# RWKV time mixing and a mixture of experts on one core: the first chunks' preparation put in another order

## What is computed

```python
h  = layernorm(x)
xk = h * mix_k + last(h) * (1 - mix_k)        # last: the token before; xv and xr likewise
k, v, r = xk @ Wk.T, xv @ Wv.T, xr @ Wr.T
wkv = wkv_log_space(exp(time_decay), time_first, k, v)   # a scan over the tokens of a sequence
x = x + layernorm((wkv * sigmoid(r)) @ Wo.T)
h2 = layernorm(x)
x = x + layernorm(routed(h2) + shared(h2))    # the best 2 of 8 experts, and a shared gated expert
```

## Time and profile before

| | |
|---|---|
| median of 3 runs | 1613.29 us (1612.08 to 1614.66) |
| the profiled execution | 1613.5 us, of which the span of its instructions is 1611.7 us |
| PE busy | 1518.8 us (94%) |
| DVE, ACT, POOL busy | 1377.9, 1335.3 and 1082.7 us (85%, 83%, 67%) |
| mean granted TensorE clock | 0.974 |

### The profile page before, as it was taken

How to read it: one execution, slowest core, us unless ns; L and a number is a source line. 1 busy time by engine, 2 the same in 40 slices (tenths; PEclk the granted TensorE clock), 3 DMA queues, 4 the chain that set the end, 5 groups by cost and what they waited for, 6 DMA issues and landing times.

```text
span 1611.7 us, 35130 instructions
## 1 busy us (share of the span) xinstructions
PE 1518.8 (94%) x9960; PEld 1363.9 (85%) x9960; DVE 1377.9 (85%) x3140; ACT 1335.3 (83%) x2768; POOL 1082.7 (67%) x1168
## 2 busy tenths in 40 slices
PE   4899999999999999999999999689999998999992
PEld 3778888888888888888888888578999998999992
DVE  4799999999999999999989988856877777999993
ACT  3688898889888998999899888756777777999993
POOL 1146767767776777677667766756666664888886
PEclk9899999999999999999999999879999999999996
DMA  3112533343322222222322222228778763777771
GB/s 112 53 47 78 169 107 125 116 153 121 109 88 87 85 78 92 87 82 80 104 76 88 81 81 69 68 79 284 237 241 249 238 217 123 233 232 228 234 236 55
DMA packets 124619, 214.41 MB, mean 133 GB/s; under 512 B 19975, under 2 KB 67338, under 8 KB 124432
## 3 DMA queue, kind: packets, MB, share of 16 engines
q1 hardware_dynamic: 92368, 126.13, 26.5%
q0 software_dynamic: 32064, 86.04, 14.5%
HBM read 116.37 MB, written 99.39 MB: 134 GB/s over the span
## 4 chain that ended last, share of the span: by engine, by line
PE 61%; POOL 16%; issue 11%; DVE 5%; ACT 2%; DMA 1%; POOLq 0%; DVEq 0%; ACTq 0%; SPq 0%
PE PS L1453 51%; POOL d_ys L589 8%; POOL out L607 6%; PE PS L1445 3%; PE PS L1517 2%; PE PS L1515 2%; PE PS L1671 2%; POOL rsw L601 1%; PE PS L1687 1%; POOL d_xd L548 1%; DMA out<-vv,wqh 0%; POOL varw L599 0%; DVE st L1060 0%; PE PS L1652 0%; PE PS L1537 0%
## 5 line engine op out<-in xcount | busy, mean ns | idle before, releaser
L548 POOL DMA_INDIRECT d_xd<-h2n,ixs x248 | 312.0, 1258 | 193.8 <-DVE h2n L1178 127.6
L1453 PE MATMUL PS<-hTh,wqh 128*128 128x512 f32 x768 | 307.1, 400 | 16.0 <-ACT kk L644 10.8
L1453 PE MATMUL PS<-hTl,wqh 128*128 128x512 f32 x768 | 306.7, 399 | 0.0
L1453 PE MATMUL PS<-hTh,wql 128*128 128x512 f32 x768 | 306.2, 399 | 0.0
L1453 PEld LDWEIGHTS PS<-hTh,wqh 128*128 128x128 f32 x768 | 146.7, 191 | 50.9 <-ACT kk L644 11.7
L1453 PEld LDWEIGHTS PS<-hTh,wql 128*128 128x128 f32 x768 | 146.6, 191 | 34.5
L1453 PEld LDWEIGHTS PS<-hTl,wqh 128*128 128x128 f32 x768 | 146.8, 191 | 33.4
L555 POOL DMA_INDIRECT d_xs<-ysh,ixs x124 | 131.2, 1058 | 45.7 <-issue 45.4
L1687 PE MATMUL PS<-weh,h2h 128*128 x380 | 106.3, 280 | 0.0
L1687 PE MATMUL PS<-weh,h2l 128*128 x380 | 106.3, 280 | 0.0
L1687 PE MATMUL PS<-wel,h2h 128*128 x380 | 106.1, 279 | 0.0
(11 more groups left out here) (328 smaller groups left out, 5715.2 us busy)
## 6 DMA issues: line engine op xcount, KB each, us to landing
xin<-in_L_attn_x SPq DMA_DIRECT2D x32, 512.0 KB, 4.2
x<-in_L_attn_x SPq DMA_DIRECT2D x32, 512.0 KB
wqh<-d_xd SPq DMA_DIRECT2D x60, 272.0 KB, 3.6
wql<-d_xd SPq DMA_DIRECT2D x60, 272.0 KB, 3.4
d_xd<-zt SPq DMA_DIRECT2D x18, 272.0 KB
wel<-in_L_ffn_w SPq DMA_DIRECT2D x16, 256.0 KB, 5.1
d_xd<-h2n,ixs POOLq DMA_INDIRECT x248, 2.5
kk<-d_xs SPq DMA_DIRECT2D x12, 256.0 KB
```

Of the source, the lines that this page charges most:

```text
L548: g.indirect_dma_start(d_xd[s], bass.IndirectOffsetOnAxis(ap=ixs[:, m % 2, k:k + 1], axis=0), h2n_of(m)[:, j, :], None).then_inc(s_sct[s], 16)
L1453: ins = mm_(out_ap, l, r, start=(k == 0), stop=(k == len(todo) - 1))
```

## The change

The instructions and transfers stay the same; only their order on SP, ACT and DVE differs, and the semaphores of two small loads.

- SP: chunk 1's rows are loaded as soon as chunk 0's are scaled, ahead of the wait for the weights (`s_wl` 6) and of `x1` and `wel`.
- ACT: `x_normed(0)` goes to the front, ahead of the three `high_mix`; `posw` and `lowb` go behind `turned_high(0)`. `x_normed(1)` goes ahead of the two waits that end the preparation. The first iterations of the loop are written out: `k_out(0)` no longer stands behind `x_normed(1)`'s place in the loop, and `beta(0)` comes ahead of `v_out(0)`, `turned_high(1)` ahead of `alpha(0)`, `own_exp(0)` and `x_normed(2)`.
- DVE: `omm` waits for its three vectors alone (`s_vec` 48; the other two count on `s_wu`). `stats_in(1)` and `negw` stand behind the last `low_mix`, ahead of the output, gate and down weights. Then `running_max(0)`, `step_up(0)`, `stats_in(2)`, `turned_low(1)`.

PE's and POOL's streams are not touched.

```diff
@@ sync
                 for i, v in enumerate((u_in, decay)):
-                    sp.dma_start(vec[:, 3 + i, :], v.rearrange("(a p) -> p a", p=P)).then_inc(s_vec, 16)
+                    sp.dma_start(vec[:, 3 + i, :], v.rearrange("(a p) -> p a", p=P)).then_inc(s_wu, 16)
...
+            sp.wait_ge(s_nx, n(0, NT, NT))
+            sp.dma_start(xin[:, :, :], x_v[1]).then_inc(s_x, 16)
             sp.wait_ge(s_wl, NP)
             sp.dma_start(x1[:, :, :], x_v[0]).then_inc(s_xr, 16)
...
-                if 0 < i < NCH:
+                if 1 < i < NCH:
                     sp.wait_ge(s_nx, n(i - 1, NT, NT))
                     sp.dma_start(xin[:, :, :], x_v[i]).then_inc(s_x, 16)
@@ scalar
-            act.wait_ge(s_vec, 16 * 5)
-            A.activation(posw[:, :], vec[:, 4, :], ACT.Exp).then_inc(s_aprep, 1)
             act.wait_ge(s_const, NCONST)
-            copy(lowb[:, :], lowf[:, :]).then_inc(s_aprep, 1)
+            x_normed(0)
             high_mix(0, al)
-            x_normed(0)
             high_mix(1, be)
             high_mix(2, ee)
             turned_high(0)
+            act.wait_ge(s_wu, 16 * 2)
+            A.activation(posw[:, :], vec[:, 4, :], ACT.Exp).then_inc(s_aprep, 1)
+            copy(lowb[:, :], lowf[:, :]).then_inc(s_aprep, 1)
...
             copy(rwp[:, :, 0:RW], rwf[:, :, :]).then_inc(s_aprep, 1)
+            x_normed(1)
 
             act.wait_ge(s_prep, 7)
             act.wait_ge(s_wl, NP)
 
-            for i in range(NCH + 2):
+            k_out(0)
+            A.preload_act_table(ACT.Silu)
+            r_tanh(0)
+            A.preload_act_table_set("natural_log_exp_and_others")
+            beta(0)
+            v_out(0)
+            turned_high(1)
+            alpha(0)
+            own_exp(0)
+            x_normed(2)
+
+            for i in range(3, NCH + 2):
@@ vector
             stats_in(0)
-            dve.wait_ge(s_vec, 16 * 5)
+            dve.wait_ge(s_vec, 16 * 3)
             V.tensor_scalar(omm[:, :, :], vec[:, 0:3, :], -1.0, 1.0, ALU.mult, ALU.add).then_inc(s_prep, 1)
-            dve.wait_ge(s_aprep, 1)
-            V.tensor_scalar(negw[:, :], posw[:, :], -1.0, None, ALU.mult).then_inc(s_prep, 1)
-            dve.wait_ge(s_prep, 2)
+            dve.wait_ge(s_prep, 1)
...
             low_mix(1)
             low_mix(2)
-
+            stats_in(1)
+            dve.wait_ge(s_aprep, 1)
+            V.tensor_scalar(negw[:, :], posw[:, :], -1.0, None, ALU.mult).then_inc(s_prep, 1)
...
-            for i in range(NCH + 2):
+            dve.wait_ge(s_prep, 2)
+            running_max(0)
+            step_up(0)
+            stats_in(2)
+            turned_low(1)
+
+            for i in range(3, NCH + 2):
                 if on(i - 5):
                     route(i - 5)
-                if on(i - 3):
+                if i > 3 and on(i - 3):
                     step_up(i - 3)
```

More of the change, by code:

```diff
@@ L209, in rwkv_moe @@
         s_vec = sem("s_vec")
+        s_wu = sem("s_wu")
         s_rwf = sem("s_rwf")
```

## The result

The changed kernel takes 1603.3 us (median of 5 runs, 1598.54 to 1604.03) against 1613.29 us (5 runs, 1612.08 to 1614.66) before: ratio 0.9931, 95% interval 0.9915 to 0.9947. That is 10.0 us faster; the forecast was 1601.8 with the range 1598.5 to 1605.5. The profiled execution took 1603.3 us.

What follows compares the result with a forecast made beforehand. PE bounds the kernel at 31.83 us per chunk from 138.60 us, so only its earlier start for chunks 0 to 2 counts; the terms sum to 11.5 us won, giving 1601.8 us, range 1598.5 to 1605.5.

Steps and rivals of the forecast that it cites:

- Step 1: Chunk 0's first projection: ACT scales the rows ahead of the weight rounding, so PE begins at 17.73, 0.65 us later.
- Step 2: Chunk 0's V: the 8.53 us wait for `kk` goes, and 2.8 us of half clock behind it.
- Step 3: Chunk 1's low part, queued behind chunk 2's rows and statistics: PE waits 3.65 us instead of 2.00, 1.7 lost.
- the upper row: Bound on chunk 2's rows' landing: 5.5 us, the longest load seen, with a megabyte ahead; the forecast took 3.9.
- chunk 2's rows come late: Rival: rows behind the experts' weights land after 5.5 us, 1.65 lost, 1603.5; first pair late too, 1604.5 to 1608.5; chance 0.16.
- Step 4: Chunks 1 and 2: waits for `rkl` (1.77) and chunk 2's low part (1.19) go; 0.4 lost to half clock.
- a new wait between 64 and 127 us: Sign on PE's timeline, at 64 to 127 us, that the prediction would be wrong.
- The sum: All steps together: -0.65 + 8.53 + 2.8 - 1.7 + 1.77 + 1.19 - 0.4 = 11.5 us won.
- given back: Rival: after chunk 2 PE meets a wait that does not move, so no change, 1613.3; chance 0.07.
- Slower: Rival: chunk 1's rows land after 19.8 us, each microsecond paid; gain gone at 31.3, 1618 at 36; chance 0.04.

Runs made afterwards that it cites:

- experiment 8: experiment 4's kernel with the third mixed weight made ahead of the first weight's low part on DVE; 1597.81 us.
- experiment 3: The changed kernel with chunk 1's low part ahead of chunk 2's statistics on DVE; 1599.9 us.
- experiment 4: The changed kernel with SP loading chunk 2's rows once chunk 1's are scaled, ahead of `x1` and the experts' weights; 1598.47 us.
- 5: The changed kernel with 22 products that nobody reads on PE ahead of chunk 1's projection; 1601.9 us.
- Experiment 6: The changed kernel with 8 products that nobody reads on PE ahead of chunk 0's second turn; 1599.53 us.
- experiment 7: The changed kernel with SP holding chunk 1's rows until the first half of chunk 0's K is done; 1608.35 us.
- experiment 9: The changed kernel once more, word for word, for a second profile; 1603.24 us.
- 1: The kernel before with only SP's early load of chunk 1's rows; 1606.65 us.
- 2: The kernel before with only ACT's and DVE's first loop iterations reordered as in the change; 1605.23 us.
- 10: experiment 8's kernel with 8 unread products on PE in each of two waits, ahead of chunk 1's projection and chunk 0's second turn; 1593.01 us.
- 11: The kernel of experiment 10 with 13 unread identity turns on PE between chunk 0's turn and the first product; 1594.68 us.
- 12: The kernel of experiment 11 once more, word for word; 1593.37 us.

## Why the prediction was right, point by point

**Step 1** (first projection 0.65 later, at 17.73): 17.83. Right, by its own mechanism, as experiment 8 showed by undoing it.

**Step 2** (V without its wait, 8.53 + 2.8): the gap is gone, and with it the half clock behind it. `wdl` starts at 26.82 (predicted 26.89), chunk 1's statistics stand at 19.86 (19.85), `kk` is copied from 27.63 (27.7), chunk 1's turn at 36.09 (36.6). The half microsecond too much is mostly the first projection, which had 7 products at the slow pace of 0.43 us instead of 9 before.

**Step 3** (chunk 1's low part, 1.7 lost) **is the term that was mis-sized**: PE waits 5.84 us where it waited 2.00, 3.8 lost. 0.6 of that is no loss, as chunk 1's turn ended at 37.1 instead of 37.7; the projection started at 42.96 instead of 41.35. The mechanism was the one named, chunk 2's rows behind the experts' weights with the low part behind them, and experiments 3 and 4 show it from both sides. The sizes were off in two places: the rows were issued at 34.76 instead of 34.0, since the first pair of weights took 5.9 us to land (27.94 to 33.84) and not 5.1 as before, and they took 39.55 - 34.76 = 4.8 us instead of 3.9; in experiments 5 to 7 they took 4.6 to 5.0. The prediction took the second pair, issued 0.9 us ahead of the rows, as mostly drained by then. In the window that ends with the rows' issue nothing had moved yet (the last figure is GB/s):

```profile
33.80:34.80 1.00, 1.00 (x6) 0.83 (x5) 0.00 (x0) 0.97 (x2) 0.00 (x0) 1.00 0.00 0
```

So the whole half megabyte was still ahead of them. The 3.87 us of the kernel before was a load with an empty queue, and in experiment 4, where the rows go ahead of the weights, they landed after 3.9 us too; the upper row, 5.5, was nearer. That is the rival "chunk 2's rows come late" at its first price: 1.6 us late at the projection against 1.65, and its time, 1603.5, lies nearer the measured one than the forecast does.

**Step 4** (1.77 + 1.19 won, 0.4 lost): both waits are gone, chunk 2's projection follows the output product without a bracket, and the `kk` wait of chunk 2 stayed (1.99, predicted 2.3). Chunk 1's projection took 19.27 us where 18.8 was taken. By chunk 2's V 10.13 us were won, 1.4 less than the sum of 11.5. A second loss had no term: the 1.88 us at chunk 0's second turn and half the clock behind it took 1.4 more, which leaves 8.73. Experiment 6 gives it back. The prediction's list of waits had no `h2n` in it (0.38 us before), and it had named a new wait between 64 and 127 us as a sign of being wrong: this one grew there.

**The sum** of 11.5 was thus 2.8 too high at the long run in this profile, and 1.5 too high in the second (9.99, experiment 9). The time came within 1.5 us of the forecast since the rest of the span was 1.5 us shorter in this execution; that part was luck and not argument. Of the rivals, "given back" was right in kind: PE, early, met waits that hang on other engines, and paid 1.4 us of clock, not 11. "Slower" had its price right up to chunk 1's projection (6.4 us there for 6.7, experiment 7) and too high behind it (3.9 us), but needed rows that land after 19.8.

## What to carry to other kernels

A wait taken away at the head of a pipe shows the next one in line, so price what each engine's queue holds behind the next transfer, and ask whether the instruction that everybody waits for needs that transfer at all: here one swapped pair of calls, or one load issued earlier, brought chunk 0's second turn 3.3 or 5.5 us forward. Don't take a load's time from a row with an empty queue if weights were issued just ahead of it. Count the clock behind a wait too: here stretches behind waits of 1.9 to 8.5 us cost another 1.3 to 2.8 us, though not every time, and work that nobody reads held the clock wherever it filled the wait. Follow a point such as the first long run's start, since the rest of the time changed by up to 4.7 us between executions, and take the clock's part out of that point as well before comparing.

## What the runs showed of the hardware

**The clock behind a wait of about 2 us is not the same each time.** At chunk 0's second turn PE stood 1.87 to 1.91 us in eight profiles. In five of them (the changed kernel twice, experiments 1, 5 and 8) the output product behind it took 3.86 to 4.36 us, in three (2, 4 and 7) 2.83. Experiment 8's window there, with both levels in it:

```profile
82.60:88.10 5.50, 5.48 (x35) 5.48 (x35) 5.04 (x8) 5.22 (x12) 2.36 (x3) 0.69 0.37 97
```

Ahead of chunk 1's projection a wait of 2.00 us was followed by slow products in the kernel before and in experiment 8, and by none in 3 and 4. At chunk 2's V, behind a wait of 1.97 to 2.30 us, 7 or 8 slow products stood in two of the 14 profiles (before and experiment 3). Behind a filled wait (one in 5 and 6, both in 10 to 12) the slow stretch was absent each time. What decides it behind an unfilled one, no run here shows. The Trainium skill (TensorE: Matmul & The Clock Gate, Part 1) says that the number of slow products at a start differs between runs of one kernel; the traces agree, with 7 and 11 such products in the first projection of the changed kernel's two profiles, and 6 to 13 over all kernels whose head was not filled. Behind the short waits no two executions of one program were seen to differ.

**The granted clock does not show all of it.** In the changed kernel's first projection the window's granted clock is 1.00, and yet its 7 products come 0.43 us apart, the pace that has 0.50 elsewhere (after the gap before V):

```profile
17.90:20.90 3.00, 3.00 (x7) 2.38 (x8) 3.00 (x6) 0.00 (x0) 0.00 (x0) 1.00 0.00 0
```

**The rest of the time goes with the clock, in part.** In the 90 us from the end of the last long run, where PE waits again, the granted clock was 0.79 with a rest of 612.9 to 614.3 us (experiments 3, 8 and 9), 0.81 with 613.8 (before), 0.83 with 610.9 to 613.6 (the changed kernel, 1, 2, 4, 5, 7, 11 and 12) and 0.87 with 609.6 and 609.8 (10 and 6). The spread of 2.7 us at 0.83 has another source, which no run here shows. Experiment 9:

```profile
1009.01:1099.01 90.00, 65.57 (x419) 59.85 (x417) 54.46 (x155) 53.02 (x111) 55.66 (x61) 0.79 0.37 124
```

and experiment 10:

```profile
1001.66:1091.66 90.00, 64.71 (x451) 59.76 (x449) 57.78 (x161) 55.64 (x116) 59.27 (x64) 0.87 0.41 138
```

The waits there are alike (the longest is 14.9 us in both); what sets the clock in them from one execution to the next, no run here shows.
